# Key and value products from 96 rows of high and low parts, and maxima turned by fp32r products with an identity

## What is computed

```python
ckv = _rms(x @ w_ckv, g_kvnorm)                       # 32 latents for each token
k_nope = (ckv @ w_dk_nope).reshape(B, T, N_HEAD, NOPE)  # 32 x 512 weights
v1 = (ckv @ w_dv).reshape(B, T, N_HEAD, V_HEAD)         # 32 x 512 weights
gate = jax.nn.softmax((x @ w_gate).mean(axis=1), axis=-1)
a1 = _attn(q, k1, v1, causal=True)    # keys k_nope and k_rope
a2 = _attn(q, ks, vs, causal=False)   # 64 selected tokens
a3 = _attn(q, kw, vw, causal=True)
out = g[:, 0] * a1 + g[:, 1] * a2 + g[:, 2] * a3
```

## Time and profile before

| | |
|---|---|
| median of 3 runs | 3019.16 us (3018.69 to 3020.45) |
| the profiled execution | 3020.62 us, its span 3018.8 us |
| mean granted TensorE clock | 0.982 |
| busy: PE, PEld, DVE, ACT, POOL | 2854.8, 2035.9, 1956.6, 1503.6, 957.6 us |
| instructions | 53729, of them 18384 products on PE |
| DMA | 91.44 MB, 30 GB/s in the mean |

### The profile page before, as it was taken

The page is one execution under the profiler, slowest core; times in us unless marked ns, Lnnn a source line. Parts: engine busy times, 40 slices in busy tenths (PEclk is TensorE's granted clock), DMA queues, the critical chain, the costliest instruction groups (busy, mean ns, idle before and its releaser), DMA issues. The chain is left out here.

```text
span 3018.8 us, 53729 instructions
## 1 busy us (share of the span) xinstructions
PE 2854.8 (95%) x18384; PEld 2035.9 (67%) x18384; DVE 1956.6 (65%) x6243; ACT 1503.6 (50%) x3228; POOL 957.6 (32%) x1764
## 2 busy tenths in 40 slices
PE   6999899999999999999999999999999999999987
PEld 4666676667766677666776667766677666776654
DVE  5666656775677656866567766667566775665654
ACT  2554344564445644465444664456544465445543
POOL 1233233432334313333133332334222332233332
PEclk7999999999999999999999999999999999999998
DMA  3111001000110001100101001110111100110000
GB/s 124 34 33 27 25 26 40 25 18 19 41 40 25 25 29 35 33 20 25 38 26 33 25 19 38 33 35 16 30 34 33 31 16 26 33 33 12 16 12 29
DMA packets 58701, 91.44 MB, mean 30 GB/s; under 512 B 19904, under 2 KB 32704, under 8 KB 58176
## 3 DMA queue, kind: packets, MB, share of 16 engines
q1 hardware_dynamic: 58432, 88.01, 9.9%
HBM read 81.68 MB, written 5.24 MB: 29 GB/s over the span
## 5 line engine op out<-in xcount | busy, mean ns | idle before, releaser
L1857 ACT ACTIVATE PR<-work 128x512 f32<-128x512 f32 (+1 forms) x1088 | 642.5, 599 | 710.7 <-PE work L1183 613.3
L1461 DVE CUSTOM_DVE_ANT_0 work<-work,KEEPB 128x128 f32<-128x128 f32 (+3 forms) x1536 | 667.2, 475 | 94.3 <-PE work L1147 93.8
L1972 POOL TENSOR_SCALAR_AFFINE_SELECT PR<-PR 128x256 f32<-128x256 f32 (+1 forms) x960 | 349.9, 369 | 709.6 <-ACT PR L1857 704.1
L1147 PE MATMUL work<-BIG 96*128 96x448 f32 (+8 forms) x1664 | 449.1, 358 | 27.9 <-DVE NMX L1461 15.0
L1181 PE MATMUL work<-BIG 99*128 99x512 f32 (+4 forms) x1152 | 422.8, 367 | 11.2 <-DVE BIG L1442 6.1
L1961 POOL TENSOR_TENSOR TOK<-AB 128x256 f32<-128x256 f32 (+1 forms) x320 | 219.0, 686 | 608.7 <-DVE AB L1423 576.7
L1218 PE MATMUL outs<-PR,ONES 128*32 128x512 f32 (+4 forms) x2304 | 404.9, 458 | 0.0
L1182 PE MATMUL work<-BIG 96*128 96x512 f32 (+4 forms) x1152 | 382.5, 332 | 0.0
L1183 PE MATMUL work<-BIG 96*128 96x512 f32 (+4 forms) x1152 | 380.8, 331 | 0.0
L1147 PEld LDWEIGHTS work<-BIG 96*128 96x128 f32 (+1 forms) x1664 | 267.8, 193 | 157.7 <-issue 78.0
L1442 DVE TENSOR_TENSOR BIG<-work,BIG 96x512 fp32r<-96x512 f32 (+1 forms) x320 | 192.1, 603 | 278.8 <-ACT BIG L1742 278.5
(11 more groups left out here) (185 smaller groups left out, 4649.8 us busy)
## 6 DMA issues: line engine op xcount, KB each, us to landing
NRM<-park SPq DMA_DIRECT2D x112, 192.0 KB, 3.1
WKW<-w_kw_dram SPq DMA_DIRECT2D x64, 256.0 KB, 2.7
WSEL<-w_sel_dram SPq DMA_DIRECT2D x64, 256.0 KB, 3.0
R<-park SPq DMA_DIRECT2D x72, 64.0 KB, 2.0
HN<-x_dram SPq DMA_DIRECT2D x8, 512.0 KB, 4.9
X<-x_dram SPq DMA_DIRECT2D x8, 512.0 KB, 3.9
out_dram<-X SPq DMA_DIRECT2D x7, 512.0 KB, 3.2
R<-park SPq DMA_DIRECT2D x16, 192.0 KB, 3.1
```

The costliest lines, as they stand in the source:

```text
L1147: last = mm(ps[:, col:col + n], q, k, start=(i_mm == 0), stop=(i_mm == len(u["mm"]) - 1))
L1461: last = v.tensor_tensor_reduce(ps[:, lo:hi], ps[:, lo:hi], KEEPB[:, T - (hi - lo):T], -1.0, -NEG, ALU.add, ALU.min, dst)
L1857: a.activation(PR[0:rows, j % NP, :], ps[0:rows, :], ACT.Exp).then_inc(exp_ready, 1)
L1972: gp.affine_select(blocks, blocks, [[0, len(cols)], [1, P]], ALU.is_ge, 0.0, base=0, channel_multiplier=-1).then_inc(exp_masked, 1)
```

## The change

- `CKVT` (128 rows, fp32) becomes `XS` of 96 rows in fp32r: high part, low part, high part of the 32 latents. ScalarE writes the two high parts (two copies of 32 x 512), VectorE writes the low part as a difference once both are there. The nope and value weights become `WN` and `WV`, 96 x 512 each in fp32r: high, high, low. They are loaded three times into `STAGE` (a view of `OT`) and split at the start: two copies of 96 x 512 by ScalarE, two differences of 32 x 512 by VectorE; TensorE waits for nv_ready ahead of the first nope. The weights of a nope or val product are now a slice of 128 columns that two pairs share, so the pair reads rows 0 or 64 on.
- `NMX` and the identity (`IDR`) become fp32r, and the four transposes of each call of `transpose_maxima` become ordinary products with the identity as the moving operand. The identity is loaded into `HT` and copied to `IDR` by VectorE at the start; TensorE waits for that copy.
- `MEANW` has 64 columns instead of 128, and the gate's steps work on 64 partitions.
- `ROW` becomes a view of the second half of `HN`, the half that holds the rotary products. So ScalarE's prologue step 4 waits for kr_ready before the copy.
- Small tensors move together or into `NRM`. The tables of times get new numbers, mostly by some tenths; one memset of 96 x 512 goes.

```diff
-        CKVT = sb("CKVT", [P, T])
+        XS = sb("XS", [3 * KVL, T], F32R)
+        WN, WV = sb("WN", [3 * KVL, 512], F32R), sb("WV", [3 * KVL, 512], F32R)
-        ROW = sb("ROW", [P, T])[:, :]
+        ROW = HN[:, 2:4, :].rearrange("p t c -> p (t c)")
+        STAGE = OT[0:3 * KVL, 2:4, :].rearrange("p n k -> p (n k)")
+        NV = [(WN[:, :], 0, 512), (WV[:, :], 512, 512)]
-        NMX = sb("NMX", [P, 2, 44])
+        NMX = sb("NMX", [P, 2, 44], F32R)
@@ sync
-        late_loads = [(WQ[0:QL, :], w_q), (WQ[QL:P, 0:1024], w_nv), (COS1[:, :, :], cos1), (SIN1[:, :, :], sin1),
+        late_loads = [(WQ[0:QL, :], w_q)] + [(STAGE[KVL * i:KVL * (i + 1), :], w_nv) for i in range(3)] + [
+                      (COS1[:, :, :], cos1), (SIN1[:, :, :], sin1),
-            sp.dma_start(ID[:, :], ident).then_inc(ident_loaded, 16)
+            sp.dma_start(HT[:, 0, 0:P], ident).then_inc(ident_loaded, 16)
@@ tensor
-                        last = mm(ps[:, 0:3], MEANW[:, :], SM[:, t, SM_W - 3:SM_W], start=(t == 0), stop=(t == NT - 1))
+                        last = mm(ps[0:64, 0:3], MEANW[:, :], SM[:, t, SM_W - 3:SM_W], start=(t == 0), stop=(t == NT - 1))
-                    last = mm(ps[:, :], WQ[:, 64 * w:64 * w + P], CKVT[:, :], start=True, stop=True)
+                    if g == 0:
+                        pe.wait_ge(nv_ready, len(NV))
+                    last = mm(ps[:, :], WN[:, P * (w // 2):P * (w // 2 + 1)], XS[:, :], start=True, stop=True)
-                        last = mm(ps[:, t * P:(t + 1) * P], CKVT[:, t * P:(t + 1) * P],
-                                  WQ[:, 512 + 64 * w:512 + 64 * w + P], start=True, stop=True)
+                        last = mm(ps[:, t * P:(t + 1) * P], XS[:, t * P:(t + 1) * P],
+                                  WV[:, P * (w // 2):P * (w // 2 + 1)], start=True, stop=True)
-                        last = nc.tensor.transpose(ps[0:35, t * P:(t + 1) * P], NMX[:, p % 2, 3 * t:3 * t + 35], ID[:, :])
+                        last = mm(ps[0:35, t * P:(t + 1) * P], NMX[:, p % 2, 3 * t:3 * t + 35], IDR[:, :], start=True, stop=True)
-                        last = nc.tensor.transpose(ps[0:2, t * P:(t + 1) * P], NMX[:, p % 2, t:8:NT], ID[:, :])
+                        last = mm(ps[0:2, t * P:(t + 1) * P], NMX[:, p % 2, t:8:NT], IDR[:, :], start=True, stop=True)
@@ vector
+                    for i, (w, c0, n) in enumerate(NV):
+                        dve.wait_ge(nv_high, i + 1)
+                        low = w[2 * KVL:3 * KVL, :]
+                        v.tensor_tensor(low, STAGE[2 * KVL:3 * KVL, c0:c0 + n], low.bitcast(F32), ALU.subtract).then_inc(nv_ready, 1)
-                    read(v.tensor_copy(CKVT[QL:P, :], ps[0:KVL, :]), "ckvT")
+                    k, _, _, r, _ = work.of["pro", n, "ckvT"]
+                    dve.wait_ge(work_read[k], r - 1)
+                    read(v.tensor_tensor(XS[KVL:2 * KVL, :], ps[0:KVL, :], XS[0:KVL, :].bitcast(F32), ALU.subtract), "ckvT")
+            dve.wait_ge(ident_loaded, 16)
+            v.tensor_copy(IDR[:, :], HT[:, 0, 0:P]).then_inc(ident_ready, 1)
-            v.memset(CKVT[0:QL, :], 0.0).then_inc(set_up, 1)
@@ scalar
+                          + [("ckvT", XS[o:o + KVL, :], lambda ps: ps[0:KVL, :]) for o in (0, 2 * KVL)]}
+                if j == 4:
+                    act.wait_ge(kr_ready, n + 1)
+                        if (layer, s) == BEGIN:
+                            act.wait_ge(late_loaded, LATE_LOADED)
+                            for w, c0, n in NV:
+                                copy(w, STAGE[:, c0:c0 + n]).then_inc(nv_high, 1)
```

Of the tables, two entries stand for the rest:

```diff
-       ("pro_act", 3, 76.46), ("pro", 3, 77.3), ("pro_pe", 6, 77.98), ("pro_act", 4, 78.2), ("pro_pe", 2, 80.26),
-       ("pro", 4, 83.26), ("pro_pe", 3, 86.16), ("pro_act", 5, 86.54), ("pro", 5, 86.95), ("pro_act", 6, 87.49),
+       ("pro_act", 3, 76.62), ("pro", 3, 77.46), ("pro_pe", 6, 77.98), ("pro_act", 4, 78.2),
+       ("pro_pe", 2, 80.26), ("pro", 4, 83.26), ("pro_pe", 3, 86.13), ("pro_act", 5, 86.83), ("pro", 5, 87.24),
```

More of the change, by code:

```diff
@@ L183, in piece_before @@
     return (k // NROPED, ROPED[k % NROPED]) if k >= 0 else None
[L189 to L190 removed]
+AFTER = [dict(pv=2.67, recip=1.83, scale=3.5, late_recip=2.31, late_scale=4.68, scale_gap=0.96, last_recip=1.54, last_scale=3.37, piece=-2.58, gap=0.65, piece_tr=2.11, max=4.98, max_gap=0.31, mt=1.82, rows=-5.38, kr=0.9, val=3.63),
+         dict(odd=3.2, lead=-5.7, lead_odd=4.53, lead_gap=0.77, lead_mt=1.84, pv=3.12, recip=1.7, scale=6.13, last_recip=0.94, last_scale=4.05, max=-0.18, max_gap=1.02, mt=2.32, piece=32.75, gap=1.06, piece_tr=1.93, kr=38.18, val=0.71)]
@@ L457, in prologue @@
                      ["pos"], ["selT"], ["imp"])[j]:
-            work.use(("pro", n, name))
+            work.use(("pro", n, name), 3 if name == "ckvT" else 1)
     def attention(layer, s):
@@ L641, in build_program @@
         RSTD = sb("RSTD", [P, 24])
-        SC, CG, CE = sb("SC", [P, NT]), sb("CG", [P, NT]), sb("CE", [P, NT])
-        MF, MB, POS = sb("MF", [P, NT]), sb("MB", [P, NT], BF16), sb("POS", [P, NT])
-        GS, GE, GG = sb("GS", [P, 3]), sb("GE", [P, 3]), sb("GG", [P, 3])
-        GM, GD = sb("GM", [P, 1]), sb("GD", [P, 3])
+        MB = sb("MB", [P, NT], BF16)
+        SMALL = sb("SMALL", [P, 45])
+        widths = [NT] * 5 + [3, 3, 3, 1, 3, 2, 2, 8]
+        SC, CG, CE, MF, POS, GS, GE, GG, GM, GD, NPART, HEAD, MHALF = \
+            (SMALL[:, sum(widths[:i]):sum(widths[:i + 1])] for i in range(len(widths)))
         WB = [ctx.enter_context(nc.psum_tensor(f"work{k}", [P, 512], F32)) for k in range(NWORK)]
@@ L1705, in _ @@
             v.memset(MHALF[:, :], -0.5).then_inc(set_up, 1)
-            for j in range(2):
-                prologue(0, j)
+            prologue(0, 0)
+            dve.wait_ge(ident_loaded, 16)
+            v.tensor_copy(IDR[:, :], HT[:, 0, 0:P]).then_inc(ident_ready, 1)
+            prologue(0, 1)
             dve.wait_ge(early_loaded, EARLY_LOADED)
```

131 lines of the change are left out of this document (64 added, 67 removed), and 12 rows, old and new, of tables (MID_A, MID_C).

## The result

| | before | after |
|---|---|---|
| median, us | 3020.08 (3018.69 to 3025.61, 6 runs) | 3034.14 (3028.12 to 3040.8, 6 runs) |
| ratio, 95% interval | 1 | 1.005 (1.004 to 1.006) |
| profiled execution: time, span | 3020.6, 3018.8 | 3036.67, 3034.6 |
| PE busy | 2854.8 | 2819.0 |
| mean granted clock | 0.982 | 0.975 |

The account below looks back on a forecast made before the run. TensorE's stream was taken as the bound: 82.6 us gross less costs of 5, 3.4, 5 and 6 leaves 63.2, so 2957.4 us from 3020.6, or 2956 against the median, rounded to 2954. The 8-in-10 range was 2930 to 2984.

Parts of the forecast that it names:

- The first step: Whole passes of both layers: TensorE is the bound, so time out of its stream leaves the span nearly one for one.
- The gross gain: TensorE's stream: nope 39.7, val 14.1, maxima 25.6 and gate 3.2 us saved, 82.6 us in all before costs.
- The sizes of the products: TensorE's pace per product: nope 0.86 to 0.24 us, val records at 0.11, maxima 0.11 to 0.06, gate 0.05 saved each.
- Waits that grow elsewhere: Cost in all passes: TensorE's stream shortens while ScalarE, GpSimd and VectorE keep their pace; 6 us, bounds 0 and some 60.
- waits absorb half: Rival: TensorE finds banks, exponentials and maxima late, losing half of 82.6 us; 2991 us, chance 0.13 (2972 to 3012).
- Its sign: Sign of waits absorb half: a long pass with PE idle for 12 us or more, waiting for VectorE or ScalarE.
- Low part of the latents: Cost in later prologues: VectorE reads the latents 3.1 us later, after three ScalarE copies; 5 us, bounds 0 and 22.
- Start: Cost ahead of the first nope: the row copy waits for `KR`, plus extra copies and differences; 5 us, between 3 and 7.
- ROW in the later prologues: Cost in the later seven prologues: ScalarE's row copy waits for `KR`, 0.5 us later each, uncovered; 3.4 us.
- The maxima: Gain in both layers: 512 transposes become identity products, from 0.11 to 0.06 us each; 25.6 us.
- The tables: New tables of times for the steps: may give back or cost 2 us each way, nothing in the sum.
- Slower by the clock: Rival for the whole run: the clock makes the kernel slower, over 3025 us; chance 0.04.

Follow-up runs that it names:

- e5: e1 with each nope product issued four times into the same bank instead of once; 3027.03 us, ratio 1.0026 to the kernel before.
- e15: The kernel before with each fp32 nope product issued twice into the same bank; 3049.18 us, ratio 1.0096.
- e1: The changed kernel with the tables of times of the kernel before, so all steps in the old order; 3021.39 us, ratio 1.0009 to the kernel before.
- e4: The kernel before with only the maxima turned by fp32r products with an identity; 3010.79 us, ratio 0.9968.
- e2: The kernel before with the changed kernel's tables of times, all products as before; 3034.5 us, ratio 1.005.
- e3: e1 with the maxima turned by transposes again, so only the latents' part is new; 3026.49 us, ratio 1.0026 to the kernel before.

## Why the prediction was wrong

- **The first step failed: that PE at 97% of a long pass makes TensorE the bound there, and that time out of its stream comes out of the span nearly one for one.** In windows of a whole pass TensorE is the busiest engine, and yet beside its stream runs a chain through ScalarE and VectorE that takes as long and sets the pace in pairs 2, 5 and 6. A microsecond of TensorE's work is worth 0.13 us by e5 and 0.55 by e15. The gross gain was to be 10.3 us a cycle (82.6 in 8); e1 has 3.1, and after the waits in pairs 7 and 8 it keeps 1 (365.0 to 364.0). The start took 4 us, and a clock of 0.978 for 0.9815 some 6.
- **The sizes of the products were right.** Nope from 0.86 to 0.23, identity products 0.06, val still 0.11, gate 0.06 from start to start; the rule of the Trainium skill's page "TensorE: Matmul & The Clock Gate" (Back-to-back issue gap, some 81 ns) stands between the two paces that the trace has, 0.06 and 0.11. Right numbers on the wrong engine.
- **"Waits that grow elsewhere", 6 us with bounds 0 and 60,** was the term that decided everything, and I took the low end because the other engines are busy for two thirds. A share of two thirds doesn't say how much of it lies in one chain: from 1184.07 to 1187.52 in e4 ScalarE has no gap at all. By the 7.2 us a cycle that e1 doesn't gain, the term was near 58 us, its upper bound. The rival "waits absorb half" named the mechanism; by e1 and e4 they took about two thirds, by e5 nearly nine tenths. Its sign came too: the pass of sequence 3 has 12 us without a PE record in the changed kernel (287.0 us long, 274.9 busy), where it had 5.8 before.
- **Low part of the latents, 5 us (0 to 22).** VectorE's delay was forecast as 3.1 us and is 3.06; its price is 1.6 us in e1's pair 8, 11 us in 7. The mechanism was right, the size half of it.
- **Start, 5 us.** 5.3 by the first exponential, of which the new order alone makes 1.4 (e2) and the products' part 3.7 (e1). The row copy starts 2.6 us later (20.84 to 23.42), VectorE's latents 3.0 (28.47 to 31.49):

```profile
23.42 0.60 ACT L1754 ACTIVATE HN<-work 128x512 f32<-128x512 f32 x1 [4.57 <-POOL KR L2023]
...
31.49 0.68 DVE L1601 TENSOR_TENSOR XS<-work,XS 32x512 fp32r<-32x512 f32 x1 [3.33 <-ACT XS L1754]
```

- **ROW in the later prologues, 3.4 us.** PE's wait for that bank went from 1.6 to 5.2 us in seven times, 3.6. That pair 7 is 0.3 to 0.5 us longer in every kernel with the change agrees. I did not try it alone.
- **The maxima, 25.6 us.** 8.7 by e4, 5 by e1 against e3, nearly all in layer 1 and the last passes, where TensorE is not covered in the same way.
- **The tables, 2 us each way, nothing in the sum.** 13 to 15 us. There was no row for it, but the diff showed which steps moved by 2.4 slots; bounds of 2 us had no ground.
- **Slower by the clock (0.04).** I asked for 142 us more of low time, since it had to cancel a gain of 65 us. The gain wasn't there, so about 44 us more in total (110.6 to 154.8 us by the profiles) are enough for the sign, at 0.30 us each and not the 0.5 that I took. The rival was priced against a sum that was itself wrong. I also wrote that TensorE waits in the stretch of the earlier trace rows; it is busy for 6.57 of its 6.80 us there, and the waiting lies in the 3.5 us ahead of it (2.72 us busy). This is the rival whose range (over 3025) the result fell into; that the lower clock makes up most of the loss is likely by the means, and why the clock falls is open.
- My last sentence on what would make it all wrong, that a part of the 0.86 us of a nope was hidden time, came closest; it was not hidden in the stream but behind ScalarE's queue.

## What to carry to other kernels

Before you count a faster product as gained, follow its result: if the reader comes to the bank more than the saving later (here 1.1 us after the product's end in most pairs, for a saving of 0.6), the product is cover, whatever the busy share of its engine says. The cheapest test is to issue the product a second time: what that costs (here 30 of 55 us) was more than making it faster brought, and issuing the fast one several times tells the rest. In a balanced kernel look first at the waits in the readers' chain; here one wait made finer gave 16 us, and all the products together nothing in the old order. Compare clocks by the means over many executions, since two profiles of one kernel differ by as much as two kernels do.

## What the hardware showed that I had not expected

- A microsecond at the lower clock costs 0.30 us over 189 executions, 0.32 over 95 cycles, and not 0.5 in this kernel (0.43 in pair 8 above). That a part of TensorE's time is cover at the low clock too would explain it; no run tests that.
- Products of 128 fp32r columns follow each other at 0.060 to 0.062 us (medians) when the weights are 2 or 35 columns wide, and at 0.113 with 128, although the loads overlap the products. The gate's fp32 products stream only 3 columns and follow each other at 0.112 with weights 128 columns wide and at 0.058 with 64. In products as short as these the narrower weights went with the faster pace.
- The mean granted clock of one and the same kernel was 0.975 in one profiled execution and 0.979 in another, with medians of 2996.7 and 2992.8 us. Over 74 executions of the kernel before it was 0.978 to 0.985.
